# Two transformer-like layers on one core: which engine multiplies what in the experts of layer 1

## The reference, cut to what matters

```python
g = jnp.einsum('th,eih->eti', x, expert_gate)            # 32 experts, inner width 64
u = jnp.einsum('th,eih->eti', x, expert_up)
outs = jnp.einsum('eti,ehi->eth', jax.nn.silu(g) * u, expert_down)
outs_t = jnp.transpose(outs, (1, 0, 2))
gathered = jnp.take_along_axis(outs_t, topk_idx[:, :, None], axis=1)
final = (gathered * topk_w[:, :, None]).sum(1)           # 8 of 32 experts per token
shared = _mlp(residuals, shared_gate, shared_up, shared_down)
return final.reshape(orig_shape) + shared
```

## Time and profile before

| | us |
|---|---|
| median of 3 runs | 1052.2 (1051.57 to 1052.24) |
| the profiled execution, its own time | 1052.27 |
| its span in the trace | 1051.0 |
| busy: PE / DVE / ACT / POOL | 997.6 / 680.0 / 506.6 / 425.9 |

### The profile page before, as it was taken

One profiled execution on the slowest core, in us unless ns is written; L12 is line 12 of the kernel. 1 busy time (PEld: TensorE's weight loads), 2 busy tenths in 40 slices (PEclk: granted clock), 3 DMA queues, 4 the chain that ended last, 5 costly groups with the idle time before them and its releaser, 6 DMA issues.

```text
span 1051.0 us, 13320 instructions
## 1 busy us (share of the span) xinstructions
PE 997.6 (95%) x4440; PEld 623.3 (59%) x4440; DVE 680.0 (65%) x1501; ACT 506.6 (48%) x1192; POOL 425.9 (41%) x336
## 2 busy tenths in 40 slices
PE   5799889799999999999999999999999999999998
PEld 2455556367555666556665675656665566656655
DVE  4846755849766587647766497665976557724933
ACT  3463573252654546454474525635266453644222
POOL 4737315454036520655108350175303652044433
PEclk9899989999999999999999999999999999999999
DMA  7140220060232302332032310323022220242061
GB/s 263 29 144 1 93 60 1 6 147 21 70 86 71 80 1 92 84 82 49 11 108 59 90 41 11 121 65 89 21 89 67 68 73 8 84 104 80 21 143 40
DMA packets 34565, 72.78 MB, mean 69 GB/s; under 512 B 4545, under 2 KB 5313, under 8 KB 34113
## 3 DMA queue, kind: packets, MB, share of 16 engines
q1 hardware_dynamic: 33072, 69.03, 24.0%
q10 hardware_dynamic: 1424, 2.90, 0.8%
HBM read 69.04 MB, written 2.88 MB: 68 GB/s over the span
## 4 chain that ended last, share of the span: by engine, by line
PE 88%; DVE 6%; issue 3%; ACT 3%; DMA 0%; POOL 0%; DVEq 0%; ACTq 0%; POOLq 0%
PE ps L692 11%; PE ps L589 11%; PE ps L453 9%; PE ps L455 9%; PE ps L454 9%; PE ps L501 6%; PE ps L514 6%; PE ps L526 5%; PE ps L667 3%; PE ps L477 3%; PE ps L484 2%; PE ps L597 2%; PE ps L638 2%; PE ps L448 1%; PE ps L493 1%
## 5 line engine op out<-in xcount | busy, mean ns | idle before, releaser
L1091 ACT ACTIVATE wide<-ps 128x512 f32<-128x512 f32 x136 | 80.9, 595 | 221.4 <-PE ps L455 220.8
L1022 ACT ACTIVATE pw<-ps,w_cols 128x512 f32<-128x512 f32 x144 | 98.8, 687 | 111.2 <-PE ps L455 109.5
L1771 POOL TENSOR_TENSOR atc<-atc,wide 128x512 f32<-128x512 f32 x64 | 82.8, 1294 | 156.4 <-DVE atc L1519 156.4
L982 ACT ACTIVATE pw<-ps,nmax 128x256 f32<-128x256 f32 x256 | 118.1, 470 | 52.8 <-DVE nmax L1319 52.7
L589 PE MATMUL ps<-pw,w_w 128*128 128x512 f32 x288 | 138.1, 603 | 0.0
L1753 POOL TENSOR_TENSOR kr<-qks,w_rope 128x512 f32<-128x512 f32 x32 | 43.5, 1360 | 194.8 <-DVE qks L1299 194.8
L1328 DVE COPY pt<-ps 128x512 f32<-128x512 f32 x128 | 85.7, 681 | 32.7 <-PE ps L514 31.7
L1390 DVE SCALAR_TENSOR_TENSOR pt<-ps,w_cols,wb 128x512 f32<-128x512 f32 x64 | 47.8, 747 | 88.0 <-PE ps L589 73.6
L514 PE MATMUL ps<-ident,pw 128*128 128x128 f32 x512 | 83.7, 287 | 21.3 <-DVE pt L1328 13.1
L1319 DVE TENSOR_REDUCE nmax<-ps 128x4 f32<-128x1024 f32 (+1 forms) x80 | 79.3, 1009 | 36.0 <-PE ps L501 35.9
L514 PEld LDWEIGHTS ps<-ident,pw 128*128 128x128 f32 x512 | 55.9, 142 | 60.9 <-issue 39.9
(11 more groups left out here) (221 smaller groups left out, 2098.3 us busy)
## 6 DMA issues: line engine op xcount, KB each, us to landing
wb<-scratch SPq DMA_DIRECT2D x128, 256.0 KB, 4.0
wb<-scratch SPq DMA_DIRECT2D x32, 512.0 KB, 5.4
wide<-scratch SPq DMA_DIRECT2D x16, 512.0 KB, 6.0
xin<-in_x SPq DMA_DIRECT2D x8, 256.0 KB, 2.7
out<-wide SPq DMA_DIRECT2D x8, 256.0 KB, 2.1
w_w<-in_w ACTq DMA_DIRECT2D x1, 1152.0 KB, 11.0
wb<-in_w SPq DMA_DIRECT2D x1, 1152.0 KB, 12.4
w_ed<-in_ed SPq DMA_DIRECT2D x1, 1024.0 KB, 17.3
```

The lines of the kernel that those rows point to most:

```text
L982: m = act.activation(pw[:, u % 2, j, :], ps[:, score_bank(u, par), qt * SEQ:(qt + 1) * SEQ], ACT.Exp, bias=nmax[:, u % 3, j:j + 1], scale= ...
L1022: act.activation(hid[:, n % 4, :], bank(UPS0[n % 2]), ACT.Gelu, bias=cols[:, C_B1 + 2 * e + c:C_B1 + 2 * e + c + 1], scale=1.0).then_inc(* ...
L1771: pool.tensor_tensor(hh[h], hh[h], sgl[:, (c + 1) % 3, :], ALU.mult).then_inc(*HH_POOL.one)
```

## The change

GpSimd no longer finishes the hidden vector; it multiplies silu of the gate with the router weight, in place in `sgl` (`weigh_gate`), for all 16 chunks. VectorE then multiplies the up product out of PSUM with that (`product1`) and thereby completes the hidden vector. The two products that VectorE did over SBUF for the last two chunks are gone. The events change accordingly: `WEIGHTED1` counts GpSimd's multiplications and frees buffers of `wb`; `HH` counts VectorE's and frees the up bank, frees `sgl`, and lets `down1` start. The core of the diff:

```diff
@@ up1, down1 (TensorE)
-                freed[bu] = HH_WEIGHED.at(s, c + 1)
+                freed[bu] = HH.at(s, c + 1)
...
-                w.wait_ge(*hh_event(s, c))
+                w.wait_ge(*HH.at(s, c + 1))
@@ weights_layer1 (SyncE), and likewise in weights_layer0
-                    w.wait_ge(*HH_WEIGHED.at(s, 1 + 2 * (n - RING) + 1))
+                    w.wait_ge(*WEIGHTED1.at(s, 2 * (n - RING) + 1))
@@ silu (ScalarE)
                 if c >= 2:
-                    w.wait_ge(*hh_event(s, c - 3))
+                    w.wait_ge(*HH.at(s, c - 2))
@@ VectorE
-            def weighted(s, c):
+            def product1(s, c):
                 h, k = (c + 1) % len(hh), UPS1[2 * ((c + 1) % 2) + 1]
                 w.wait_ge(*UP.at(s, c + 1))
                 if c < 0:
                     w.wait_ge(*DOWN.at(s - 1))
                     w.wait_ge(*SILU.at(s, 0))
-                    dve.tensor_tensor(hh[h], bank(k), sgl[:, 0, :], ALU.mult).then_inc(*HH_WEIGHED.one)
-                    return
+                else:
+                    w.wait_ge(*WEIGHTED1.at(s, c))
                 if c >= 5:
                     w.wait_ge(*DOWN.at(s, c - 5))
-                w.wait_ge(*wb_layer1(c // 2, s))
-                dve.tensor_tensor(hh[h], bank(k), wb[:, c % (2 * RING), :], ALU.mult).then_inc(*HH_WEIGHED.one)
-                if c >= CH1 - 2:
-                    w.wait_ge(*SILU.at(s, c + 1))
-                    w.wait_ge(*HH_WEIGHED.at(s, c + 1))
-                    dve.tensor_tensor(hh[h], hh[h], sgl[:, (c + 1) % 3, :], ALU.mult).then_inc(*HH_DVE.one)
+                dve.tensor_tensor(hh[h], bank(k), sgl[:, (c + 1) % 3, :], ALU.mult).then_inc(*HH.one)
@@ GpSimd
-            def gate_hidden(s, c):
-                h = (c + 1) % len(hh)
-                w.wait_ge(*HH_WEIGHED.at(s, c + 1))
+            def weigh_gate(s, c):
                 w.wait_ge(*SILU.at(s, c + 1))
-                pool.tensor_tensor(hh[h], hh[h], sgl[:, (c + 1) % 3, :], ALU.mult).then_inc(*HH_POOL.one)
+                w.wait_ge(*wb_layer1(c // 2, s))
+                pool.tensor_tensor(sgl[:, (c + 1) % 3, :], sgl[:, (c + 1) % 3, :], wb[:, c % (2 * RING), :],
+                                   ALU.mult).then_inc(*WEIGHTED1.one)
@@ experts1 (GpSimd), and likewise for the tail
-                for c in range(8, CH1 - 2):
-                    gate_hidden(x, c)
+                for c in range(8, CH1):
+                    weigh_gate(x, c)
```

More of the change, by code:

```diff
@@ L285, in two_layers @@
             "v1", "v1_biased", "v1_silu", "qk1", "kernel1", "kv1", "gated"))
-        GATE, SILU, UP, HH_WEIGHED, DOWN = (event(n, CH1 + 1) for n in (
-            "gate", "silu", "up", "hh_weighed", "down"))
-        HH_POOL, HH_DVE = event("hh_pool", CH1 - 2), event("hh_dve", 2)
+        GATE, SILU, UP, HH, DOWN = (event(n, CH1 + 1) for n in ("gate", "silu", "up", "hh", "down"))
+        WEIGHTED1 = event("weighted1", CH1)
         GATED_OUT, LAY1, ROWS1, OUT_ROWS = event("gated_out"), event("lay1"), event("rows1"), event("out_rows")
@@ L361, in weights_layer0 @@
                     elif s:
[L362 removed]
+                        w.wait_ge(*WEIGHTED1.at(s - 2, 2 * (RING + k) + 1))
                     src = bass.AP(tensor=scratch0.tensor, offset=2 * k * TOK,
@@ L377, in weights_layer1 @@
                 else:
-                    w.wait_ge(*HH_WEIGHED.at(s - 1, 1 + 2 * (RING + k) + 1))
+                    w.wait_ge(*WEIGHTED1.at(s - 1, 2 * (RING + k) + 1))
                 for par in range(2):
@@ L392, in denominators @@
                     w.wait_ge(*GATED.at(s - 1))
-                w.wait_ge(*HH_POOL.at(s - 2))
-                w.wait_ge(*HH_DVE.at(s - 2))
+                w.wait_ge(*HH.at(s - 2))
                 w.wait_ge(*OUT.at(s - 2))
@@ L1084, in silu @@
                 if c >= 2:
-                    w.wait_ge(*hh_event(s, c - 3))
-                else:
-                    if s < LAST:
-                        w.wait_ge(*NORMALISED.at(s + 1))
-                    if s:
-                        w.wait_ge(*hh_event(s - 1, (14, 15, 13)[c + 1]))
+                    w.wait_ge(*HH.at(s, c - 2))
+                elif s < LAST:
+                    w.wait_ge(*NORMALISED.at(s + 1))
+                else:
+                    w.wait_ge(*HH.at(s - 1))
                 act.activation(sgl[:, (c + 1) % 3, :], bank(UPS1[2 * ((c + 1) % 2)]), ACT.Silu).then_inc(*SILU.one)
@@ L1642, in experts1 @@
                 x, n, more = s - 1, s + 1, s < LAST
-                weighted(x, -1)
+                product1(x, -1)
                 x1_rows(s, 6)
-                weighted(x, 0)
+                product1(x, 0)
                 variance1(s)
-                weighted(x, 1)
+                product1(x, 1)
                 if more:
                     y0_low(n, 3)
-                weighted(x, 2)
+                product1(x, 2)
                 shifts(1, s)
-                weighted(x, 3)
-                weighted(x, 4)
+                product1(x, 3)
+                product1(x, 4)
                 if more:
@@ L1657, in experts1 @@
                     variance0(s + 2)
-                weighted(x, 5)
-                weighted(x, 6)
+                product1(x, 5)
+                product1(x, 6)
                 if s + 2 < STEPS:
@@ L1663, in experts1 @@
                 swap1(s, 1)
-                weighted(x, 7)
+                product1(x, 7)
                 v1_bias(s, 0, 6)
                 rope1_add(s, 0)
-                weighted(x, 8)
+                product1(x, 8)
                 v1_bias(s, 1, 3)
                 rope1_add(s, 1)
-                weighted(x, 9)
+                product1(x, 9)
                 route1_scores(s)
-                weighted(x, 10)
+                product1(x, 10)
                 kernel1(s, 0, 6)
@@ L1675, in experts1 @@
                 route1_groups(s)
-                weighted(x, 11)
+                product1(x, 11)
                 if more:
@@ L1681, in experts1 @@
                     route1_mask(s)
-                weighted(x, 12)
+                product1(x, 12)
                 gate1(s, 0, 3)
@@ L1686, in experts1 @@
                     route1_top(s)
-                weighted(x, 13)
+                product1(x, 13)
                 if not more:
                     route1_weights(s)
-                weighted(x, 14)
+                product1(x, 14)
                 if more:
                     maxima(n, 0)
-                weighted(x, 15)
+                product1(x, 15)
                 y1_low(s)
@@ L1718, in dve_program @@
             for c in range(-1, CH1):
-                weighted(LAST, c)
+                product1(LAST, c)
             out_rows(LAST, 4)
@@ L1870, in experts1 @@
                 x = s - 1
-                gate_hidden(x, 0)
+                weigh_gate(x, 0)
                 power(1, s)
                 for c in range(1, 6):
-                    gate_hidden(x, c)
+                    weigh_gate(x, c)
                 if s + 2 < STEPS:
                     power(0, s + 2)
-                gate_hidden(x, 6)
+                weigh_gate(x, 6)
                 rope1_turn(s, 0)
-                gate_hidden(x, 7)
+                weigh_gate(x, 7)
                 rope1_turn(s, 1)
-                for c in range(8, CH1 - 2):
-                    gate_hidden(x, c)
+                for c in range(8, CH1):
+                    weigh_gate(x, c)
                 if s < LAST:
@@ L1900, in pool_program @@
             shortcut(LAST)
-            for c in range(CH1 - 2):
-                gate_hidden(LAST, c)
+            for c in range(CH1):
+                weigh_gate(LAST, c)
         sp_program()
```

5 lines of the change are left out of this document (removed).

## The result

| | before | after |
|---|---|---|
| median, us | 1051.9 (1051.36 to 1052.24, 4 runs) | 1061.4 (1059.45 to 1062.59, 4 runs) |
| the profiled execution, its own time | 1052.27 | 1059.45 |
| its span | 1051.0 | 1058.1 |

The change makes the kernel slower: ratio 1.0089, interval 1.0072 to 1.0106. The forecast was 1058.2 with a range of 1053.6 to 1062.0. The sign and the places of most stalls were right, the sum was 3 us short. The forecast's own range, 1055 to 1061, doesn't reach the median; the wider one does.

What follows compares the result with a forecast made beforehand. The prediction took TensorE as the bound (busy 95% of the span, 88% of the last-ending chain). Its terms, 1.5 + 1.4 + 1.7 + 0.8 + 0.5 = 5.9 us on 1052.27, gave 1058.2; range 1053.6 to 1062, own range 1055 to 1061.

Steps and rivals of the forecast that it cites:

- Term 1: Middle mixed stage, first part: `shifts` 1.5 us late uses up the lead of `z1_cols`, just in time; 0 us taken.
- Term 2: Middle mixed stage, rotary part: VectorE's additions and GpSimd's products take turns at SBUF, delaying `qk1`; 0.3 us a stage.
- Term 3: First mixed stage: late router weights now hold GpSimd too; 1.1 us down the `z1_cols` chain plus 0.3 rotary, 1.4.
- Term 4: Last mixed stage: 0.6 us at `z1_cols`, 0.3 rotary, 0.3 routing, 0.5 at its end; together 1.7.
- Term 5: Start of the tail: GpSimd's product and a hand-over come ahead of VectorE, delaying the down product; 0.8 us.
- Term 6: End of the kernel: VectorE's product of the last chunk now follows GpSimd's and ends later than before; 0.5 us.
- A: Rival: TensorE's lead hides all stage terms, only forced chains of 1.8 us remain, 1054.1 us; chance 0.16.
- B: Rival: GpSimd and VectorE lock up, costing 1.0 us more in each of five middle stages, 1063 us; chance 0.17.
- C: Rival: VectorE's relief gives back up to 1.48 us of the last mixed stage's routing wait, 1050.7 us; chance 0.05.

Runs made afterwards that it cites:

- e7: Changed kernel with VectorE's `shifts` moved ahead of `product1` of chunk 1, run for a trace; the same kernel was timed at 1059.7 us, ratio 1.0064.
- e3: Changed kernel with each rotary addition on VectorE (`rope1_add`) placed one chunk's product earlier; 1059.6 us, ratio 1.0066.
- e1: The changed kernel run once more, unaltered, for its trace; 1063.3 us, ratio 1.0096 to the kernel before.
- e6: Changed kernel with the edits of e7, e3 and e4 together; 1055.4 us, ratio 1.0033 to the kernel before.
- e9: e6 with chunk 0 of each round wholly as in the kernel before; 1053.1 us, ratio 1.0008 to the kernel before.
- e4: Changed kernel with both products of chunks 14 and 15 on VectorE again, as before the change; 1059.3 us, ratio 1.0063.

## Why the prediction was right, and where it was short

- *Term 1, middle stage, first part: 0 (to 0.1) taken, 0.16 to 0.19 measured.* The walk is right to 0.07 us at every step (above). "Just in time" should have been priced: a lead of 1.3 us used up by a shift of 1.5 is not zero. e7 shows that it is this chain.
- *Term 2, rotary part: 0.3 taken, 0.28 to 0.29 measured* in four stages, nothing in the fifth. The turns at SBUF came as walked, and e3 removes the wait by moving the turn. By the Trainium skill (SBUF — State Buffer, "Who interferes with whom") two SBUF inputs on VectorE contend with a GpSimd instruction that reads SBUF; the runs agree, and show that the price is the rest of GpSimd's product whatever the size of VectorE's: 1.24 us for 128 x 8, 1.26 against 0.29 for 128 x 128.
- *Five middle stages: 1.5 taken, 2.1 measured:* 0.9 more by term 1, 0.3 less by term 2.
- *Term 3, first mixed stage: 1.4 taken, 1.6 measured in e1.* The place was only partly right: most of it, 0.97, is the up product of chunk 3 waiting for chunk 1's bank, not `uv`. The late weights delay chunk 0 and through `power` chunk 1, whose bank TensorE wants before it comes to `uv`; the margin of 0.3 that term 1 found there was smaller than the 1.1 of this stage.
- *Term 4, last mixed stage: 1.7 taken, 3.0 measured: the step that was mis-sized.* The first part, 0.6 taken at `uv`, cost nothing there and 0.28 + 0.70 at the banks of the up products of chunks 3 and 5. The 0.28 hangs on chunk 0, as in the first stage: it stays in e6 and is gone in e9. The 0.70 hangs on `shifts`: the walk followed them to `z1_cols` and left out silu of chunk 3, which stands behind `z1_rows` on ScalarE and holds up GpSimd, VectorE and the bank; e7 removes it. The routing, 0.3 taken with bounds of -0.5 and 1.0, cost 1.07: the prediction allowed that operations might escape GpSimd's turns, but one of 0.29 us met a whole GpSimd product of a chunk that had been VectorE's before (e4). The rotary part, 0.3 taken, cost 0.42, and the end 0.54, as taken.
- *Term 5: 0.8 taken, 0.6 measured* (0.7 in e1). *Term 6: 0.5 taken, 0.54 measured.*
- *The sum was 5.9, the stalls of e1 come to 7.9, and the clock, which has no term at all, adds 3.2 us there;* five of e1's six executions have its granted clock of 0.987. Of the four executions of the result one has 0.987, and the profiled one no such stretch; for the other two, at 0.989, it isn't shown. It is a knock-on of terms 4 and 5: both lengthen a wait of TensorE late in the kernel, from 1.48 to 2.54 and from 1.07 to 2.33 us. That the median still lies inside the range is in part luck: e1's, of the same kernel, is 1063.3, outside it.
- *Rivals.* A, only forced chains, falls with e7 and e3. B's time of 1063 is near e1's median, but its mechanism isn't there: the middle stages grow by 0.47 or less, not 1.3. C, relief of VectorE in the last stage, went the other way: that wait grew.

## What to carry to other kernels

Moving a product between engines is priced by what stands behind it in the waiting engine's written order: here thirteen chunks of the new form cost less than 1 us between the traces once `shifts`, the rotary additions, chunk 0 and the last two chunks were placed well. Follow a late result to everything that stands behind its reader, too: silu of chunk 3 behind `z1_rows` was the stall that the walk missed. Where a second engine's long operation over SBUF is put beside a stretch of small ones on VectorE, price one whole long operation, not a share. When a change lengthens a TensorE wait that already exists, look at the granted clock behind it in several executions, not in one profile; the fastest may be the one without it.
